# Edge MLP of a four-layer graph network: the stages of TensorE moved two groups apart, with two PSUM banks each, and another release for the gathers on GpSimd

## Chip, cores and metric

One core of one Trainium2 chip runs the whole program. The metric is the device time of one execution in microseconds (us); the figure for a kernel is the median over several executions.

## What is computed

The reference runs four graph layers over 6250 nodes (128 features) and 100000 edges sorted by destination. After each layer comes a residual sum and a layer norm. The change touches the third layer only, the edge MLP:

```
row, col = src, dst
e = silu(concat(h[row], h[col]) @ We1 + be1)     # 256 -> 64
e = silu(e @ We2 + be2)                          # 64 -> 64
agg = segment_sum(e, row)
out = silu(concat(h, agg) @ Wn1 + bn1) @ Wn2 + bn2
```

## The kernel before, in words

`h @ We1` is done per node ahead of this stage, so for an edge only two table rows are added: one half is looked up by a matmul from a table in SBUF (`look2`, three bf16 parts), the other half is fetched by an indirect DMA from the table `t2` in DRAM. The stage works in groups of eight tiles of 128 edges. There are 98 groups of tiles to gather (`CTILE_GROUPS`) and 104 groups of steps to compute (`CSTEP_GROUPS`), because a tile that spans two windows of nodes is used in more than one step. The gathered rows lie in a ring of 12 groups (`CRING`); a row of the ring may be overwritten once the step group five back (`LAG`) has read it. The engines run the same list of groups, each in its own order, and are held together by semaphores alone:

- **GpSimd (POOL)**, L1798 to L1809: for each tile group it waits for a semaphore `l2_placed`, then for the landing of the group two back (`landed`, L1776), and then issues eight indirect DMAs (L1804).
- **VectorE (DVE)**, L1928 to L1974: `hot_look` (L1931, one tensor_scalar in bf16 of 1024 columns) makes the one-hot matrix for the lookup; `before_silu` (L1942, eight additions) waits for the gather of its group and adds it to the looked-up half; `hot_sum` (L1948, one tensor_tensor in f32 of 1024 columns, both inputs in SBUF) makes the one-hot matrix for the sums; `add` (L1958) adds a window of sums to the accumulator.
- **TensorE (PE)**, L1866 to L1921: `own_half` (L1873, 24 matmuls in bf16), `turn` (L1883, four transposes), `second_product` (L1888 for the bias, L1892 for the product), `summed` (L1899 to clear the window, L1904 for the sums, L1906 to close).
- **ScalarE (ACT)**, L1825 to L1860: `silu1` (L1834), `keep_silu1` (L1839), the second silu (L1847), and the copies that place the indices of a later group (L1826, L1829), after which `l2_placed` rises.
- **SyncE (SP)**, L1812 to L1821: loads the rows for `hot_look`, two groups at a time.

`conv_rounds` (L1766) writes the first round of twelve groups out, puts the full rounds in a hardware loop, and writes out what remains. The order within a step is written by hand. Before, in step k:

```
PE:   own_half(k+2), turn(k+1), second_product(k), summed(k-1)
ACT:  silu1(k+1), keep_silu1(k+1), second silu(k), place(k+6)
DVE:  hot_look(k+3), before_silu(k+2), hot_sum(k), add(k-1)
```

`turn` and `second_product` have one PSUM bank each (`ST`, `EB`), `own_half` and `summed` two each. The next stage starts when the last step of all engines is done. The graph convolutions (`convolution`, L2176) use `conv_rounds` and `landed` too.

Of the kernel before, what the change touches and what calls it, by code (L numbers as in the profile page):

```python
# [21 lines left out]
ACT = mybir.ActivationFunctionType  # L22
# [18 lines left out]
CG = 8  # L41
CRING = 12
CSLOTS = CG * CRING
CSTEP_GROUPS = STEPS // CG
CTILE_GROUPS = -(-ET // CG)
CROUNDS = CSTEP_GROUPS // CRING
LAG = -(-(CSLOTS - CG - USED) // CG)
# [45 lines left out]
def build(nc, x, edge_i, edge_f, W_att_w, W_att_b, W1_w, W1_b, W2_w, W2_b, a_vec,  # L93
# [3 lines left out]
    with ctx:  # L97
# [63 lines left out]
        junk = sb("junk", [P, 2, G * D])  # L161
# [5 lines left out]
        ident = sb("ident", [P, P])  # L167
# [27 lines left out]
        we2 = sb("we2", [P, P])  # L195
# [44 lines left out]
        at = [0]  # L240
# [6 lines left out]
        bias2 = tab_rows(CG * EH // 2, 3).bitcast(BF16)  # L247
# [1515 lines left out]

        def conv_rounds(eng, body, groups):  # L1766

            for g in range(CRING):
                body(0, g, g)
            with eng.Fori(1, groups // CRING) as i:  # L1770
                for g in range(CRING):
                    body(i, g, i * CRING + g)
            for k in range(groups // CRING * CRING, groups):
                body(k // CRING, k % CRING, k)

        def landed(pool, i, g, k):  # L1776
# [5 lines left out]
        def at_least(eng, signal, k, more):  # L1782

            if not isinstance(k, int) or k + more > 0:
                eng.wait_ge(signal, k + more)
# [1 line left out]
        (l2_placed, l2_hotT, l2_look, l2_pre, l2_s1, l2_s1T, l2_s1T_kept, l2_e, l2_s2, l2_same, l2_sum, l2_acc) = (  # L1787
            sem(f"l2_{n}") for n in ("placed", "hotT", "look", "pre", "silu1", "silu1T", "silu1T_kept", "e", "silu2", "hot_sum", "sum", "acc"))
        l2_rel_in = [sem(f"l2_rel_in{n}") for n in range(2)]
        LB, ST, EB = bank[0:2], bank[2], bank[4]  # L1790
        with nc.Block() as block:
            def from_group(k, back):

                return 1 + (max(0, k - back) if isinstance(k, int) else k - back)

            @block.gpsimd
            def _(pool):
                def step(i, g, k):  # L1798
                    pool.wait_ge(l2_placed, from_group(k, LAG))
                    landed(pool, i, g, k)  # L1800
                    pool.sem_inc(rounds, 1)
                    for u in range(CG):
                        slot = g * CG + u
                        q_.indirect_dma_start(mlp_ring[:, slot * EH:(slot + 1) * EH], None, t2, bass.IndirectOffsetOnAxis(  # L1804
                            ap=idx_now[:, slot:slot + 1].bitcast(U32), axis=0)).then_inc(conv_gathered[g], 16)

                pool.wait_ge(t2_out[0], 16 * ((NB + 1) // 2))
                pool.wait_ge(t2_out[1], 16 * (NB // 2))
                conv_rounds(pool, step, CTILE_GROUPS)  # L1809
# [13 lines left out]
            @block.scalar  # L1823
            def _(act):
                def place_tiles(k, g):  # L1825
                    return s_.copy(idx_now[:, g * CG:(g + 1) * CG], dst2_t[:, bass.ds(k * CG, CG)])  # L1826

                def place_steps(k, g):
                    return s_.copy(rel_now[:, g * CG:(g + 1) * CG], rel2[:, bass.ds(k * CG, CG)])  # L1829

                def silu1(k, g):
                    act.wait_ge(l2_pre, k + 1)
                    at_least(act, l2_s1T, k, -1)
                    s_.activation(junk[:, g % 2, :], pre_now[:, g % 2, :, :].rearrange("p u f -> p (u f)"), ACT.Silu).then_inc(l2_s1, 1)  # L1834

                def keep_silu1(k, g):
                    act.wait_ge(l2_s1T, k + 1)
                    at_least(act, l2_e, k, -1)
                    s_.copy(s1T[:, g % 2, :], ST).then_inc(l2_s1T_kept, 1)  # L1839

                def step(i, g, k):
                    if not isinstance(k, int) or k + 1 < CSTEP_GROUPS:
                        silu1(k + 1, g + 1)
                        keep_silu1(k + 1, g + 1)
                    act.wait_ge(l2_e, k + 1)
                    at_least(act, l2_sum, k, -1)
                    s_.activation(s2[:, g % 2, :], EB, ACT.Silu).then_inc(l2_s2, 1)  # L1847
                    if not isinstance(k, int) or k + LAG + 1 < CTILE_GROUPS:
                        place_tiles(k + LAG + 1, (g + LAG + 1) % CRING)
                    if not isinstance(k, int) or k + LAG + 1 < CSTEP_GROUPS:  # L1850
                        at_least(act, l2_same, k, LAG + 2 - CRING)
                        place_steps(k + LAG + 1, (g + LAG + 1) % CRING).then_inc(l2_placed, 1)

                for k in range(LAG + 1):
                    place_tiles(k, k)
                    last = place_steps(k, k)
                last.then_inc(l2_placed, 1)
                silu1(0, 0)
                keep_silu1(0, 0)
                conv_rounds(act, step, CSTEP_GROUPS)  # L1860

            @block.tensor
            def _(pe):
                nodes, offsets = ([pe.alloc_register(f"l2_{n}{u}") for u in range(CG)] for n in ("look", "offset"))

                def own_half(k, g):  # L1866
                    pe.reg_load(nodes, step2_node[0:1, bass.ds(k * CG, CG)])
                    pe.wait_ge(l2_hotT, k + 1)
                    at_least(pe, l2_pre, k, -1)
                    for u in range(CG):  # L1870
                        node = pe.snap(nodes[u], min_val=0, max_val=NT - 1)
                        for c in range(3):
                            last = t_.matmul(LB[g % 2][:, u * EH:(u + 1) * EH], hotT8[:, g % 2, u * P:(u + 1) * P],  # L1873
                                             flat(look2[:, bass.ds(node, 1), c * EH:(c + 1) * EH]), start=(c == 0), stop=(c == 2))
                    last.then_inc(l2_look, 1)

                def turn(k, g):
                    pe.wait_ge(l2_s1, k + 1)
                    at_least(pe, l2_s1T_kept, k, 0)
                    pe.sem_inc(rounds, 1)  # L1880
                    for u in range(CG // 2):
                        at = slice(u * P, (u + 1) * P)
                        last = t_.transpose(ST[:, at], junk[:, g % 2, at], ident[:, :])  # L1883
                    last.then_inc(l2_s1T, 1)

                def second_product(k, g):
                    at_least(pe, l2_s2, k, 0)
                    t_.matmul(EB, ones3, bias2, start=True, stop=False)  # L1888
                    pe.wait_ge(l2_s1T_kept, k + 1)
                    for u in range(CG // 2):  # L1890
                        at = slice(u * P, (u + 1) * P)
                        last = t_.matmul(EB[:, at], s1T[:, g % 2, at], we2[:, :], start=False, stop=(u == CG // 2 - 1))  # L1892
                    last.then_inc(l2_e, 1)

                def summed(k, g):
# [10 lines left out]
                    t_.matmul(window[:, 0:2], zeros2[:, 0:P], zeros2[:, 0:2], start=False, stop=True).then_inc(l2_sum, 1)  # L1906

                def step(i, g, k):
                    if not isinstance(k, int) or k + 2 < CSTEP_GROUPS:
                        own_half(k + 2, g + 2)  # L1910
                    if not isinstance(k, int) or k + 1 < CSTEP_GROUPS:
                        turn(k + 1, g + 1)
                    second_product(k, g)
                    if not isinstance(k, int) or k > 0:
                        summed(k - 1, g - 1 + CRING)

                own_half(0, 0)
                own_half(1, 1)
                turn(0, 0)
                conv_rounds(pe, step, CSTEP_GROUPS)  # L1920
                summed(CSTEP_GROUPS - 1, CSTEP_GROUPS - 1)  # L1921

            @block.vector
            def _(dve):
# [18 lines left out]
                    last.then_inc(l2_pre, 1)  # L1943

                def hot_sum(k, g):
                    dve.wait_ge(l2_placed, from_group(k, LAG))
                    at_least(dve, l2_sum, k, -1)
                    v.tensor_tensor(out=hot8[:, g % 2, :, :], in0=iota[:, :].unsqueeze(1).to_broadcast([P, CG, P]),  # L1948
                                    in1=rel_now[:, g * CG:(g + 1) * CG].unsqueeze(2).to_broadcast([P, CG, P]),
                                    op=ALU.is_equal).then_inc(l2_same, 1)  # L1950
# [7 lines left out]
                    v.tensor_add(here, here, bank[6 + g % 2].rearrange("p (t f) -> p t f", t=CG)).then_inc(l2_acc, 1)  # L1958

                def step(i, g, k):  # L1960
                    if not isinstance(k, int) or k + 3 < CSTEP_GROUPS:
                        hot_look(i, g + 3, k + 3)
                    if not isinstance(k, int) or k + 2 < CSTEP_GROUPS:
                        before_silu(i + (g + 2) // CRING, (g + 2) % CRING, k + 2)
                    hot_sum(k, g)
                    if not isinstance(k, int) or k > 0:
                        add(k - 1, g - 1 + CRING)

                for k in range(3):
                    hot_look(0, k, k)  # L1970
                for k in range(2):
                    before_silu(0, k, k)
                conv_rounds(dve, step, CSTEP_GROUPS)
                add(CSTEP_GROUPS - 1, CSTEP_GROUPS - 1)  # L1974
        for k in range(CTILE_GROUPS):
            conv_count[k % CRING] += 16 * CG

# [460 lines left out]
```

## Time and profile before

| | us |
|---|---|
| median of 3 runs | 5702.95 (5699.57 to 5705.49) |
| the profiled execution | 5707.85 |
| its span in the trace | 5706.1 |

| engine | busy us | share of the span |
|---|---|---|
| PE | 3351.8 | 59% |
| PE weight load | 2787.7 | 49% |
| DVE | 2996.6 | 53% |
| ACT | 1491.7 | 26% |
| POOL | 3889.4 | 68% |

The edge MLP's edge stage lies between 2432 and 3507 us of the span. Shares of the whole span say little of it, as the program has many stages with different limits, one after another. The indirect DMAs of a stage count as busy time of POOL for as long as POOL works on issuing them; the transfer itself comes after.

### The profile page before, as it was taken

How to read it: one execution, taken by the hardware profiler on the slowest of the kernel's cores; microseconds unless marked ns; L12 is line 12 of the kernel's file. 1: busy time of each engine (PE TensorE's matmuls, PEld its weight loads, DVE VectorE, ACT ScalarE, POOL GpSimd, SP SyncE). 2: the span in 40 equal slices, each digit the busy share in tenths (PEclk: the TensorE clock that was granted, in tenths of full speed). 3: DMA queues.
4: the chain of work that ended last, by engine and by line, in shares of the span. 5: the costliest groups of instructions: out<-in, count | busy, mean ns of one | idle time of the engine just before them, and what ended most of it. 6: DMA issues, size and time to landing. Idle time of an engine off the chain costs nothing. (4 is left out here: it accounts for less than half of the span.)

```text
span 5706.1 us, 80490 instructions
## 1 busy us (share of the span) xinstructions
PE 3351.8 (59%) x17155; PEld 2787.7 (49%) x17156; DVE 2996.6 (53%) x10412; ACT 1491.7 (26%) x5625; POOL 3889.4 (68%) x4054
## 2 busy tenths in 40 slices
PE   4444444366666666779999999444444454444443
PEld 3333333355655556667777777333333343333333
DVE  6887777577777787733333333333333343333335
ACT  2334333345555555511111113100000000000001
POOL 3777777727777777377777770577777747777773
PEclk7555555577788787855555556655555565655555
DMA  4222112224444444121111110111111121111111
GB/s 123 54 53 53 53 53 56 48 62 132 132 130 131 131 132 130 52 61 53 53 53 53 53 53 11 52 53 52 52 52 52 52 56 53 53 52 52 52 52 52
DMA packets 220198, 386.15 MB, mean 68 GB/s; under 512 B 83394, under 2 KB 119824, under 8 KB 219940
## 3 DMA queue, kind: packets, MB, share of 16 engines
q0 software_dynamic: 142944, 296.35, 19.0%
q1 hardware_dynamic: 76996, 86.71, 4.9%
q8 instruction: 119, 1.95, 0.1%
q14 instruction: 139, 1.14, 0.1%
HBM read 356.23 MB, written 26.56 MB: 67 GB/s over the span
## 5 line engine op out<-in xcount | busy, mean ns | idle before, releaser
L2187 POOL DMA_INDIRECT arena<-table_gcn,idx_now x1568 | 1491.1, 951 | 717.0 <-issue 418.4
L2234 PE MATMUL pair<-arena,hotf 128*128 x3328 | 755.6, 419 | 1095.3 <-DMA arena<-table_gcn,idx_now 1094.0
L2234 PEld LDWEIGHTS pair<-arena,hotf 128*128 128x128 f32 x3328 | 705.6, 322 | 1240.0 <-issue 1239.9
L655 POOL DMA_INDIRECT arena<-table_attention,idx_now x832 | 811.9, 976 | 271.1 <-issue 193.2
L655 POOL DMA_INDIRECT arena<-table_key_value,idx_now x832 | 788.7, 948 | 276.3 <-issue 220.6
L2261 DVE TENSOR_TENSOR acc<-acc,pair 128x1024 f32 x208 | 253.8, 1220 | 1342.5 <-PE pair L2237 1342.4
L1804 POOL DMA_INDIRECT arena<-table_edge_mlp,idx_now x784 | 754.9, 963 | 261.5 <-issue 214.0
L1043 PE MATMUL pair<-wide,hotf 128*128 128x130 f32 x1664 | 430.9, 439 | 630.4 <-ACT wide L1007 620.9
L1043 PEld LDWEIGHTS pair<-wide,hotf 128*128 128x128 f32 x1664 | 369.1, 326 | 695.5 <-ACT wide L1007 685.8
L2196 ACT COPY idx_now<-src_t 128x8 int32 (+1 forms) x204 | 39.3, 197 | 1876.9 <-PE pair L2237 1865.7
L1942 DVE TENSOR_TENSOR hot<-pair,arena 128x64 f32<-128x64 f32 x832 | 134.0, 224 | 640.0 <-DMA arena<-table_edge_mlp,idx_now 619.1
L1376 PE MATMUL pair<-wide,hotf 128*128 128x132 f32 x1664 | 316.3, 349 | 231.6 <-DVE acc L1406 231.6
L2251 DVE TENSOR_SCALAR hotf<-iota,rel_now,ew_now 128x128 f32<-128x128 f32 x1664 | 444.8, 367 | 7.4 <-ACT ew_now L2201 7.4
L1376 PEld LDWEIGHTS pair<-wide,hotf 128*128 128x128 f32 x1664 | 269.5, 243 | 271.9 <-issue 269.8
L1904 PEld LDWEIGHTS pair<-wide,hotf 128*128 128x128 f32 x1664 | 359.4, 328 | 45.0 <-issue 45.0
L1904 PE MATMUL pair<-wide,hotf 128*128 128x64 f32 x1664 | 378.9, 422 | 0.0
L1367 PE MATMUL pair<-arena 128*128 x1664 | 312.1, 351 | 8.7 <-DVE arena L1423 8.5
L1367 PEld LDWEIGHTS pair<-arena 128*128 128x128 f32 x1664 | 297.5, 268 | 9.2 <-issue 9.2
L1319 ACT ACTIVATE junk<-iota,rel_now 128x128 f32<-128x128 f32 x832 | 265.7, 390 | 18.3 <-ACT idx_now L643 12.6
L1007 ACT ACTIVATE wide<-arena,small 128x129 f32<-128x129 f32 x832 | 267.0, 393 | 0.0
L918 DVE SCALAR_TENSOR_TENSOR junk<-iota,rel_now,arena 128x128 f32<-128x128 f32 x832 | 256.9, 344 | 0.0
L1438 DVE TENSOR_TENSOR junk<-pair,arena 128x512 f32<-128x512 f32 x208 | 143.8, 691 | 204.5 <-DMA arena<-table_key_value,idx_now 204.4
(366 smaller groups left out, 5586.6 us busy)
## 6 DMA issues: line engine op xcount, KB each, us to landing
key<-rel_dram SPq DMA_DIRECT2D x104, 256.0 KB, 3.5
arena<-rel_dram SPq DMA_DIRECT2D x52, 512.0 KB, 3.7
arena<-table_gcn,idx_now POOLq DMA_INDIRECT x1568, 2.5
arena<-table_attention,idx_now POOLq DMA_INDIRECT x832
arena<-table_key_value,idx_now POOLq DMA_INDIRECT x832
arena<-table_edge_mlp,idx_now POOLq DMA_INDIRECT x784, 2.4
table_attention<-arena SPq DMA_DIRECT2D x13, 512.0 KB, 2.9
table_gcn<-acc SPq DMA_DIRECT2D x26, 256.0 KB, 2.3
```

Of the source, the lines that this page charges most:

```text
L655: q_.indirect_dma_start(ring[:, slot, 0:width], None, table, bass.IndirectOffsetOnAxis(ap=idx_now[:, slot:slot + 1].bitcast(U32), axis=0)) ...
L918: last = v.scalar_tensor_tensor(out=junk[:, 0, u * P:(u + 1) * P], in0=iota[:, :], scalar=rel_now[:, g * G + u:g * G + u + 1], in1=dst_sco ...
L1007: last = s_.activation(wide[:, g, u, 0:D + 1], ring[:, g * G + u, 0:D + 1], ACT.Identity, scale=small[:, g, u:u + 1])
L1043: last = t_.matmul(bank[2 * (g % 2) + u // 2][:, (u % 2) * AW:(u % 2) * AW + D + 2], hotf[:, g, u, :], wide[:, g, u, 0:D + 2], start=True, ...
L1319: last = s_.activation(away[:, u * P:(u + 1) * P], iota[:, :], ACT.Abs, scale=-1.0, bias=rel_now[:, g * G + u:g * G + u + 1])
L1367: last = t_.matmul(QB[g % 2][:, u * P:(u + 1) * P], hotT_f[:, g, u * P:(u + 1) * P], flat(look[:, bass.ds(nodes[u], 1), :]), start=True, s ...
L1376: last = t_.matmul(bank[SUM + 2 * (g % 2) + u // 2][:, (u % 2) * AW:(u % 2 + 1) * AW], hotf[:, g, u, :], wide[:, g, u, :], start=True, sto ...
L1804: q_.indirect_dma_start(mlp_ring[:, slot * EH:(slot + 1) * EH], None, t2, bass.IndirectOffsetOnAxis(ap=idx_now[:, slot:slot + 1].bitcast(U ...
L1904: t_.matmul(window[:, bass.ds(offset * EH, EH)], hot8[:, g % 2, u, :], s2[:, g % 2, u * EH:(u + 1) * EH], start=False, stop=False)
L2187: q_.indirect_dma_start(conv_ring[:, slot * D:(slot + 1) * D], None, table, bass.IndirectOffsetOnAxis(ap=idx_now[:, slot:slot + 1].bitcast ...
L2234: t_.matmul(window[:, bass.ds(offset * D, D)], hot8[:, g % 2, u, :], conv_ring[:, bass.ds(slot * D, D)], start=False, stop=False)
L2251: last = v.tensor_scalar(out=hot8[:, g % 2, u, :], in0=iota[:, :], scalar1=rel_now[:, at], scalar2=ew_now[:, at], op0=ALU.is_equal, op1=AL ...
```

## The change

PE's four parts stand two groups apart in place of one; `ST` and `EB` become two banks each, taken in turn; ACT and DVE follow with their own order. Indices are placed eight groups ahead (`PLACED`) in place of six, and POOL waits for `l2_pre` (the additions of L1942 of the group five back) in a wait of its own. On DVE `before_silu` now comes first in a step and `hot_look` second, in front of `hot_sum`; its last loop round is written out. In step k after the change:

```
PE:   own_half(k+4), turn(k+2), second_product(k), summed(k-2)
ACT:  keep_silu1(k+2), second silu(k), silu1(k+4), place(k+8)
DVE:  before_silu(k+4), hot_look(k+6), hot_sum(k), add(k-2)
```

```diff
-        def conv_rounds(eng, body, groups):
+        def conv_rounds(eng, body, groups, unrolled_rounds=0):
...
-            with eng.Fori(1, groups // CRING) as i:
+            looped = groups // CRING - unrolled_rounds
+            with eng.Fori(1, looped) as i:
...
-            for k in range(groups // CRING * CRING, groups):
+            for k in range(looped * CRING, groups):
...
-        LB, ST, EB = bank[0:2], bank[2], bank[4]
+        LB, ST, EB = bank[0:2], bank[2:4], bank[4:6]
+        PLACED = 8
...
-                    pool.wait_ge(l2_placed, from_group(k, LAG))
+                    pool.wait_ge(l2_placed, from_group(k, PLACED - 1))
+                    if not isinstance(k, int) or k >= LAG:
+                        pool.wait_ge(l2_pre, k - LAG + 1)
...
+                    if not isinstance(k, int) or k + 2 < CSTEP_GROUPS:
+                        keep_silu1(k + 2, g + 2)
                     act.wait_ge(l2_e, k + 1)
                     at_least(act, l2_sum, k, -1)
-                    s_.activation(s2[:, g % 2, :], EB, ACT.Silu).then_inc(l2_s2, 1)
+                    s_.activation(s2[:, g % 2, :], EB[g % 2], ACT.Silu).then_inc(l2_s2, 1)
+                    if not isinstance(k, int) or k + 4 < CSTEP_GROUPS:
+                        silu1(k + 4, g + 4)
+                    if not isinstance(k, int) or k + PLACED < CTILE_GROUPS:
+                        place_tiles(k + PLACED, (g + PLACED) % CRING)
...
-                for k in range(LAG + 1):
+                for k in range(PLACED):
                     place_tiles(k, k)
                     last = place_steps(k, k)
...
-                    at_least(pe, l2_s1T_kept, k, 0)
+                    at_least(pe, l2_s1T_kept, k, -1)
...
-                    at_least(pe, l2_s2, k, 0)
+                    at_least(pe, l2_s2, k, -1)
...
+                    if not isinstance(k, int) or k + 4 < CSTEP_GROUPS:
+                        own_half(k + 4, g + 4)
                     if not isinstance(k, int) or k + 2 < CSTEP_GROUPS:
-                        own_half(k + 2, g + 2)
-                    if not isinstance(k, int) or k + 1 < CSTEP_GROUPS:
-                        turn(k + 1, g + 1)
+                        turn(k + 2, g + 2)
                     second_product(k, g)
-                    if not isinstance(k, int) or k > 0:
-                        summed(k - 1, g - 1 + CRING)
+                    if not isinstance(k, int) or k >= 2:
+                        summed(k - 2, g - 2 + CRING)
...
-                    if not isinstance(k, int) or k + 3 < CSTEP_GROUPS:
-                        hot_look(i, g + 3, k + 3)
-                    if not isinstance(k, int) or k + 2 < CSTEP_GROUPS:
-                        before_silu(i + (g + 2) // CRING, (g + 2) % CRING, k + 2)
+                    if not isinstance(k, int) or k + 4 < CSTEP_GROUPS:
+                        before_silu(i + (g + 4) // CRING, (g + 4) % CRING, k + 4)
+                    if not isinstance(k, int) or k + 6 < CSTEP_GROUPS:
+                        hot_look(i, g + 6, k + 6)
                     hot_sum(k, g)
-                    if not isinstance(k, int) or k > 0:
-                        add(k - 1, g - 1 + CRING)
+                    if not isinstance(k, int) or k >= 2:
+                        add(k - 2, g - 2 + CRING)
...
-                conv_rounds(dve, step, CSTEP_GROUPS)
-                add(CSTEP_GROUPS - 1, CSTEP_GROUPS - 1)
+                conv_rounds(dve, step, CSTEP_GROUPS, 1)
+                for k in range(CSTEP_GROUPS - 2, CSTEP_GROUPS):
+                    add(k, k)
```

## Rows read from the trace of the kernel before

**Rows 1.** Stretches: length; busy PE, PEld, DVE, ACT, POOL; PEclk, DMA share, GB/s

```profile
2434.00:3430.00 996.00, 905.38 (x5329) 738.22 (x5330) 341.66 (x1064) 193.17 (x483) 754.93 (x784) 0.51 0.20 54
3430.00:3507.00 77.00, 73.45 (x397) 60.48 (x395) 27.66 (x80) 12.80 (x24) 0.00 (x0) 0.50 0.02 8
```

**Rows 2.** The gathers' line L1804: duration min/median/max, then what POOL waited for

```profile
L1804 POOL DMA_INDIRECT arena<-table_edge_mlp,idx_now x784: 940/944/1994, 2434.2 to 3426.8; - x196
...
  issue: 214.0, 702
  DMA arena<-table_edge_mlp,idx_now: 24.7, 81
```

**Rows 3.** Waits of the stage, 2420 to 3470 us: total, times, longest

```profile
DVE hot L1942 <- DMA arena<-table_edge_mlp,idx_now: 619.1, 96, 8.7
...
PE pair L1883 <- ACT junk L1834: 83.1, 82, 5.7
```

**Rows 4.** Timeline of ACT, the first of the copies that place indices: start, duration

```profile
2431.98 0.20 ACT L1826 COPY idx_now<-tab 128x8 int32<-128x8 int32 x1 [1.65 <-PEq L1529]
```

**Rows 5.** Timeline of POOL and DVE, an ordinary group

```profile
3389.30 1.28 DVE L1942 TENSOR_TENSOR hot<-pair,arena 128x64 f32<-128x64 f32 x8 [6.42 <-DMA arena<-table_edge_mlp,idx_now]
3390.43 0.94 POOL L1804 DMA_INDIRECT arena<-table_edge_mlp,idx_now  x1 [0.30 <-issue]
3390.50 1.22 DVE L1948 TENSOR_TENSOR hotf<-iota,rel_now 128x1024 f32<-128x1024 f32 x1
...
3391.68 0.94 POOL L1804 DMA_INDIRECT arena<-table_edge_mlp,idx_now  x1 [0.30 <-issue]
3392.24 0.64 DVE L1931 TENSOR_SCALAR hotT<-arena,part 128x1024 bf16<-128x1024 bf16 x1
```

**Rows 6.** The same timeline where a gather is stretched: two groups

```profile
2557.56 1.22 DVE L1948 TENSOR_TENSOR hotf<-iota,rel_now 128x1024 f32<-128x1024 f32 x1
2558.31 1.29 POOL L1804 DMA_INDIRECT arena<-table_edge_mlp,idx_now  x1 [0.30 <-issue]
...
2617.53 1.22 DVE L1948 TENSOR_TENSOR hotf<-iota,rel_now 128x1024 f32<-128x1024 f32 x1
2617.57 1.99 POOL L1804 DMA_INDIRECT arena<-table_edge_mlp,idx_now  x1 [0.30 <-issue]
```

**Rows 7.** Timeline: hot_look straight behind the additions, in the first groups

```profile
2456.91 0.94 POOL L1804 DMA_INDIRECT arena<-table_edge_mlp,idx_now  x1 [0.30 <-issue]
2456.94 0.48 DVE L1931 TENSOR_SCALAR hotT<-arena,part 128x1024 bf16<-128x1024 bf16 x1
```

**Rows 8.** Timeline behind the last gather: DVE and PE

```profile
3431.01 1.28 DVE L1942 TENSOR_TENSOR hot<-pair,arena 128x64 f32<-128x64 f32 x8 [8.02 <-DMA arena<-table_edge_mlp,idx_now]
...
3433.09 1.09 PE L1883 MATMUL pair<-ident,junk 128*128 128x128 f32 x4 [2.39 <-ACT junk L1834]
...
3433.93 0.48 DVE L1931 TENSOR_SCALAR hotT<-arena,part 128x1024 bf16<-128x1024 bf16 x1
...
3434.33 1.13 DVE L1942 TENSOR_TENSOR hot<-pair,arena 128x64 f32<-128x64 f32 x8
```

**Rows 9.** Timeline of PE, one step of the end

```profile
3461.79 0.60 PE L1888 MATMUL pair<-tab 3*128 3x512 bf16 x1
...
3464.33 0.60 PE L1899 MATMUL pair<-wide 1*128 1x512 bf16 x1
...
3468.59 1.46 PE L1873 MATMUL pair<-arena,hotT 128*128 x24
```

**Rows 10.** PE's groups of instructions from 3431 to 3507 us

```profile
L1904 PE MATMUL pair<-wide,hotf 128*128 128x64 f32 x144 | 33.1, 425 | 0.0
L1892 PE MATMUL pair<-we,tab 128*128 128x128 f32 x64 | 16.6, 441 | 0.0
```

**Rows 11.** Timeline of the transposes of the next stage, at either clock level

```profile
3508.68 1.12 PE L2061 MATMUL pair<-ident,x_nodes 128*128 128x128 f32 x4
...
3520.56 0.60 PE L2061 MATMUL pair<-ident,x_nodes 128*128 128x128 f32 x4
```

More of the change, by code:

```diff
@@ L1838, in keep_silu1 @@
                     at_least(act, l2_e, k, -1)
-                    s_.copy(s1T[:, g % 2, :], ST).then_inc(l2_s1T_kept, 1)
+                    s_.copy(s1T[:, g % 2, :], ST[g % 2]).then_inc(l2_s1T_kept, 1)
                 def step(i, g, k):
-                    if not isinstance(k, int) or k + 1 < CSTEP_GROUPS:
-                        silu1(k + 1, g + 1)
-                        keep_silu1(k + 1, g + 1)
+                    if not isinstance(k, int) or k + 2 < CSTEP_GROUPS:
+                        keep_silu1(k + 2, g + 2)
                     act.wait_ge(l2_e, k + 1)
                     at_least(act, l2_sum, k, -1)
-                    s_.activation(s2[:, g % 2, :], EB, ACT.Silu).then_inc(l2_s2, 1)
[L1848 to L1852, printed above, removed]
-                for k in range(LAG + 1):
+                    s_.activation(s2[:, g % 2, :], EB[g % 2], ACT.Silu).then_inc(l2_s2, 1)
[3 more added lines that the diff above has]
+                        place_tiles(k + PLACED, (g + PLACED) % CRING)
+                    if not isinstance(k, int) or k + PLACED < CSTEP_GROUPS:
+                        at_least(act, l2_same, k, PLACED + 1 - CRING)
+                        place_steps(k + PLACED, (g + PLACED) % CRING).then_inc(l2_placed, 1)
+                for k in range(PLACED):
                     place_tiles(k, k)
@@ L1858, in _ @@
                 silu1(0, 0)
+                silu1(1, 1)
                 keep_silu1(0, 0)
+                silu1(2, 2)
+                keep_silu1(1, 1)
+                silu1(3, 3)
                 conv_rounds(act, step, CSTEP_GROUPS)
@@ L1882, in turn @@
                         at = slice(u * P, (u + 1) * P)
-                        last = t_.transpose(ST[:, at], junk[:, g % 2, at], ident[:, :])
+                        last = t_.transpose(ST[g % 2][:, at], junk[:, g % 2, at], ident[:, :])
                     last.then_inc(l2_s1T, 1)
                 def second_product(k, g):
-                    at_least(pe, l2_s2, k, 0)
-                    t_.matmul(EB, ones3, bias2, start=True, stop=False)
+                    at_least(pe, l2_s2, k, -1)
+                    t_.matmul(EB[g % 2], ones3, bias2, start=True, stop=False)
                     pe.wait_ge(l2_s1T_kept, k + 1)
@@ L1891, in second_product @@
                         at = slice(u * P, (u + 1) * P)
-                        last = t_.matmul(EB[:, at], s1T[:, g % 2, at], we2[:, :], start=False, stop=(u == CG // 2 - 1))
+                        last = t_.matmul(EB[g % 2][:, at], s1T[:, g % 2, at], we2[:, :], start=False, stop=(u == CG // 2 - 1))
                     last.then_inc(l2_e, 1)
@@ L1908, in step @@
                 def step(i, g, k):
+                    if not isinstance(k, int) or k + 4 < CSTEP_GROUPS:
+                        own_half(k + 4, g + 4)
                     if not isinstance(k, int) or k + 2 < CSTEP_GROUPS:
-                        own_half(k + 2, g + 2)
-                    if not isinstance(k, int) or k + 1 < CSTEP_GROUPS:
-                        turn(k + 1, g + 1)
+                        turn(k + 2, g + 2)
                     second_product(k, g)
-                    if not isinstance(k, int) or k > 0:
-                        summed(k - 1, g - 1 + CRING)
+                    if not isinstance(k, int) or k >= 2:
+                        summed(k - 2, g - 2 + CRING)
                 own_half(0, 0)
@@ L1919, in _ @@
                 turn(0, 0)
+                own_half(2, 2)
+                turn(1, 1)
+                own_half(3, 3)
                 conv_rounds(pe, step, CSTEP_GROUPS)
-                summed(CSTEP_GROUPS - 1, CSTEP_GROUPS - 1)
+                for k in range(CSTEP_GROUPS - 2, CSTEP_GROUPS):
+                    summed(k, k)
             @block.vector
@@ L1945, in hot_sum @@
                 def hot_sum(k, g):
-                    dve.wait_ge(l2_placed, from_group(k, LAG))
+                    dve.wait_ge(l2_placed, from_group(k, PLACED - 1))
                     at_least(dve, l2_sum, k, -1)
@@ L1960, in step @@
                 def step(i, g, k):
-                    if not isinstance(k, int) or k + 3 < CSTEP_GROUPS:
-                        hot_look(i, g + 3, k + 3)
-                    if not isinstance(k, int) or k + 2 < CSTEP_GROUPS:
-                        before_silu(i + (g + 2) // CRING, (g + 2) % CRING, k + 2)
+                    if not isinstance(k, int) or k + 4 < CSTEP_GROUPS:
+                        before_silu(i + (g + 4) // CRING, (g + 4) % CRING, k + 4)
+                    if not isinstance(k, int) or k + 6 < CSTEP_GROUPS:
+                        hot_look(i, g + 6, k + 6)
                     hot_sum(k, g)
-                    if not isinstance(k, int) or k > 0:
-                        add(k - 1, g - 1 + CRING)
-                for k in range(3):
+                    if not isinstance(k, int) or k >= 2:
+                        add(k - 2, g - 2 + CRING)
+                for k in range(2):
                     hot_look(0, k, k)
-                for k in range(2):
+                for k in range(4):
                     before_silu(0, k, k)
-                conv_rounds(dve, step, CSTEP_GROUPS)
-                add(CSTEP_GROUPS - 1, CSTEP_GROUPS - 1)
+                    hot_look(0, k + 2, k + 2)
+                conv_rounds(dve, step, CSTEP_GROUPS, 1)
+                for k in range(CSTEP_GROUPS - 2, CSTEP_GROUPS):
+                    add(k, k)
         for k in range(CTILE_GROUPS):
```

## The prediction

> **What bounds the kernel now.** I read the page for the place of the stage, then its busy time by stretch, then the waits, then the timeline of a few groups. In the stretch with the gathers POOL is busy 754.9 of 996 us, and PE 905.4 [rows 1]. That looks like a bound on PE, but the waits say otherwise. Of POOL's 783 gaps between gathers (98 groups of eight) 702 are called issue, 214.0 us, and 81 are put down to a landing, 24.7 us: 0.305 us each in both cases [rows 2]. A real wait would make the second kind longer; it doesn't, so POOL never waits after its first start, and it runs at 0.944 + 0.305 = 1.25 us per gather, about 10.0 us per group. DVE waits 619.1 us for landings, and PE waits 83.1 us for the first silu, which hangs on these landings [rows 3]. So POOL sets the pace up to its last gather, 3426.8 + 0.9 us [rows 2]. Behind that PE works off what is left: 73.5 of 77 us busy [rows 1].
>
> This splits the change into three terms: when POOL starts, how fast it runs, and how much PE has left when the last rows have landed.
>
> **Start.** Eight groups of indices are placed before the first signal in place of six: four more copies, each 0.2 us long [rows 4]. ACT's copies can overlap, so this costs between 0 and 0.8 us; I take +0.4. Nothing hides it, as POOL's first gather waits for the last of them.
>
> **POOL's extra wait.** Its wait for `l2_pre` of the group five back was met long ago: DVE adds a group as soon as it lands, and POOL itself waits for the landing of the group two back. Behind it on POOL are the eight gathers, and behind these DVE. The gap at a group's first gather, which holds two waits and an increment, is 0.305 us like the others [rows 2]. A third wait: 0, at most 0.01 us x 98 = 1 us. The index copies are moved from six to eight groups ahead, but now stand behind silu1(k+4), which ACT can only do when group k+4 has landed; POOL asks for group k+8 then four groups later, so 30 us are left. SP's row loads keep their distance of three groups to `hot_look`: 0. DVE's written-out round adds instructions to an engine that waits 619.1 us for landings [rows 3]: 0.
>
> **DVE's new order and POOL.** This is the term that I find largest. An ordinary gather takes 0.944 us, but 784 of them take 754.9, so 754.9 - 740.1 = 14.8 us are stretch [rows 1, 2]. The timeline shows whose. Where a gather starts while `hot_sum` (L1948) is running, it ends 0.81 us after `hot_sum` does: started 0.04 us into it, it takes 1.99 (2617.57 + 1.99 = 2619.56, against 2618.75); started 0.75 into it, 1.29 [rows 6]. Today the phases mostly just miss: over all 98 groups the timeline has 28 stretched gathers, one in a group at most. The additions start when the group lands, `hot_sum` 1.20 us later, 0.07 behind a gather's start; the next gather starts 1.18 into it, when 0.04 is left, and takes 0.94 [rows 5].
>
> After the change `hot_look` stands between. Straight behind the additions it starts at 1.19 and takes 0.48, with a gather started 0.03 before it that keeps its 0.94 [rows 7]; the next DVE instruction follows 0.40 after it [rows 8]. So `hot_sum` starts 1.60 us after the additions, 0.47 after a gather's start at 1.13 [rows 5], and the next gather falls 0.78 into it with 0.44 left. The nearest row is the one started 0.75 into it: 1.29 us, +0.34 [rows 6]. That is for 97 groups (the last has no gather behind it) 33 us. In seven groups of 98 (the first pair of [rows 6] is of one) the landing comes so late that `hot_look` itself starts about 0.55 behind a gather's start and is held, as in the ordinary group of today (0.64 in place of 0.48 [rows 5]); there about 0.96 is lost in place of 0.34, 4 us more. From the 37 goes today's 14.8: **+22 us**. As the loss is what is left of `hot_sum`, each 0.1 us of phase is worth 0.1 us per group, 10 us in all. I take that for both ends, since it is the distance by which today's groups miss: +12 and +32.
>
> The page "SBUF — State Buffer" of the Trainium skill, section "Who interferes with whom", says that a DVE instruction with two SBUF inputs contends with a GpSimd instruction that reads SBUF, and one in a 2-port mode with any, and that the second to come is blocked for the whole of the first. Its first half agrees with the 1.99 [rows 6]; by the second half a gather could be held through `hot_look` too, which is a rival below.
>
> **What PE has left.** PE gains nothing in the stretch of the gathers: its 83.1 us of waiting [rows 3] move from `turn` to `own_half`, which needs the additions of the group two back for its bank. At the end it costs. When group 97 is added (3431.01), PE today has `second_product` 96 to 103, eight of them, and `summed` 95 to 103, nine, before it: 64 and 144 instructions [rows 10], with seven `turn` and five `own_half`. After the change `own_half(99)` waits for that addition, in step 95. Behind it are the same `turn` and `own_half`, but `second_product` 95 to 103 and `summed` 93 to 103: one and two more. A `second_product` is 3464.33 - 3461.79 = 2.54 us, a `summed` 3468.59 - 3464.33 = 4.26 [rows 9], together 11.1. PE starts 2.08 us after the addition today (3433.09 [rows 8]), then about 1.9, behind `hot_look`. **+10.9 us**. Nothing covers it: PE has no gap in that stretch. Second banks for `ST` and `EB` remove no wait there, since PE runs without one: 0.
>
> **Sum.** 0.4 + 22 + 10.9 = +33 us. The profiled execution took 5707.85 us (span 5706.1), 4.9 above the median of the runs; on the median of 5702.95 the sum gives 5736. Own range of this case: 5722 to 5750.
>
> **Rivals.**
> 1. The gathers are stretched no more than today (a gather slips in between `hot_look` and `hot_sum`, or the landing phase moves). For it: 70 of 98 groups miss, mostly by 0.1 us,, so phases are fine things. Against: the stretch follows the phase in every row. Time: 5703 + 11.3 = 5714. Chance 0.12.
> 2. `hot_look`, near a gather, is itself held, until 1.19 us after the gather's start, as where it starts 0.56 behind (3391.68 to 3392.88 [rows 5]). Then `hot_sum` starts just before the next gather, and that takes 1.9: 97 x 0.95 = 92, less 15, plus 11.3: 5791. Against: 0.48 at 0.03 behind the start [rows 7]. Chance 0.05.
> 3. One hold over both DVE instructions: the gather begun at 1.13 waits from 1.20 to 2.82 and takes 0.81 more, 2.5 us in place of 0.94: 97 x 1.56 = 151, less 15, plus 11.3: 5850. Against: that gather keeps 0.94 beside `hot_look` [rows 7]. Chance 0.02. [...]
> 4. The other side: TensorE's granted clock rises from its lower level (1.2 GHz) to its upper (2.4) in PE's last stretch. Four transposes take 1.12 us at the one and 0.60 at the other [rows 11]. That stretch has 73.5 us of PE's work today [rows 1] and 84 with the 10.9 more; it would take 45: 5736 - 39 = 5697, and 5675 together with rival 1. It decides once some 70 of the 84 us run at the upper level. Against: PE was busy without a gap there today, and the granted clock was 0.50 all through [rows 1]. Chance 0.05. The page "TensorE: Matmul & The Clock Gate" of the Trainium skill, section "What's actually happening", says that activity releases the throttle; by this rule today's stretch should have run at the upper level, and it did not.
> 5. The change does nothing that can be seen, the waits and banks being slack on both sides: 5703. Chance 0.04.
>
> **How the numbers follow.** My case has 0.72. A difference under 0.2% (11.4 us) is about what a measurement of this kernel can't tell from none: 5691.5 to 5714.4. Rival 1 lies on that edge, half on each side; rival 4 goes 0.03 to faster and 0.02 to same; rival 5 is same. Faster 0.03, same 0.12, slower 0.85. The range takes my case and rival 1: 5712 to 5752, and leaves out rivals 2 to 5 and the ends of mine, 0.2.
>
> **What would show it.** Right: POOL's first start within 1 us of today's; 784 gathers with a mean near 990 ns and a median near 944, one in eight about 1.28; issue gaps still 0.3; DVE still waiting for landings; PE's wait now at L1873; from the last additions behind a landing to the stage's end 86 in place of 75 us, with 72 instructions of L1892 and 176 of L1904 in it, at a granted clock of 0.50. Wrong: a mean of the gathers at or under 963 ns, waits of POOL on DVE or ACT, or a last stretch of the old length.

## The result and the profile after

The changed kernel took 5746.18 us (median of 6, 5741.98 to 5753.52) against 5703.94 us for the kernel before: ratio 1.0074, 95% interval 1.0062 to 1.0085. It is 42 us slower; the forecast was 33 us slower (5736, range 5712 to 5752). A second measurement on another chip gave 5754.55 against 5708.23, ratio 1.0082 (1.0068 to 1.0096), and there the kernel before compared with itself gave 1.0000 (0.9991 to 1.0009). The profiled execution has a span of 5745.2 us against 5706.1.

Busy time of the changed kernel by stretch: first the gathers, then what follows them (columns: length; busy PE, PE weight load, DVE, ACT, POOL with their counts; granted clock, DMA share, GB/s).

```profile
2437.00:3461.00 1024.00, 991.42 (x5282) 795.73 (x5283) 332.01 (x1059) 179.37 (x474) 783.36 (x784) 0.50 0.19 52
3461.00:3551.00 90.00, 87.81 (x440) 72.31 (x439) 31.08 (x85) 14.85 (x31) 0.00 (x0) 0.50 0.02 7
```

Against [rows 1] the first stretch is 28 us longer and the second 13. POOL's busy time grew by as much as its stretch did, 754.9 to 783.4. The view of the gathers' line (now L1808) shows that nothing but their duration changed:

```profile
L1808 POOL DMA_INDIRECT arena<-table_edge_mlp,idx_now x784: 940/944/1932, 2437.2 to 3458.2; - x196
...
  issue: 220.0, 722
  ACT rel_now L1833: 23.2, 1
  DMA arena<-table_edge_mlp,idx_now: 18.6, 61
```

The gaps are 0.305 us each as in [rows 2], the median is still 944 ns, and there is one real wait, the first. From the first gather's start to the last one's are 1021.0 us in place of 992.6, which is +28.4, and 28.4 is also what the busy time grew by (783.4 - 754.9). The timeline of an ordinary group in the hardware loop shows the stretch:

```profile
2970.76 1.28 DVE L1955 TENSOR_TENSOR hot<-pair,arena 128x64 f32<-128x64 f32 x8 [6.87 <-DMA arena<-table_edge_mlp,idx_now]
2971.90 0.94 POOL L1808 DMA_INDIRECT arena<-table_edge_mlp,idx_now  x1 [0.30 <-issue]
2972.03 0.49 DVE L1944 TENSOR_SCALAR hotT<-arena,part 128x1024 bf16<-128x1024 bf16 x1
2972.43 1.22 DVE L1961 TENSOR_TENSOR hotf<-iota,rel_now 128x1024 f32<-128x1024 f32 x1
2973.14 1.32 POOL L1808 DMA_INDIRECT arena<-table_edge_mlp,idx_now  x1 [0.30 <-issue]
```

The gather that starts beside `hot_look` (L1944) keeps its 0.94, as [rows 7] had it. The next one starts 0.71 us into `hot_sum` (L1961) and ends 0.81 us after it: 2974.46 against 2973.65. That is the rule of [rows 6]. Over the whole stage 91 gathers, in 97 groups that have a next one, start 0.04 to 1.06 us into `hot_sum`, and each of them ends 0.80 to 0.82 us after it; four more take 1.01 to 1.05 us. Before, 28 gathers started there.

The rest lies behind the last gather. The lines are the additions of the last gathered group and the last `add` of the changed kernel, then the last `add` of the kernel before:

```profile
3462.41 0.23 DVE L1955 TENSOR_TENSOR hot<-pair,arena 128x64 f32<-128x64 f32 x1 [8.48 <-DMA arena<-table_edge_mlp,idx_now]
...
3550.03 0.69 DVE L1971 TENSOR_TENSOR acc<-acc,pair 128x512 f32 x1 [3.48 <-PE pair L1915]
```

```profile
3505.90 0.69 DVE L1958 TENSOR_TENSOR acc<-acc,pair 128x512 f32 x1 [3.48 <-PE pair L1906]
```

DVE adds that group 4.2 us after the gather's start, as in [rows 8]; from there to the end of the last `add` (3550.72) it is 88.3 us, before 3506.59 - 3431.01 = 75.6: +12.7. The spans differ by 39.1 us: 28.4 and 12.7, and 3.0 by which the first gather comes later (the stages ahead and the first copies), less some 5 that the stages behind took less.

### The profile page after: what moved, and what is told of

The parts are those of the page before. It is cut to its first block and busy times, and to the rows that moved or that the text cites. A ratio compares the mean times of both kernels' runs of the same rounds, so it can differ in the third digit from the quotient of the medians.

```text
span 5745.2 us, 80504 instructions
## 1 busy us (share of the span) xinstructions
PE 3442.7 (60%) x17155; PEld 2849.1 (50%) x17156; DVE 2990.5 (52%) x10412; ACT 1480.1 (26%) x5627; POOL 3919.8 (68%) x4054
## 5 line engine op out<-in xcount | busy, mean ns | idle before, releaser
L1808 POOL DMA_INDIRECT arena<-table_edge_mlp,idx_now x784 | 783.4, 999 | 261.8 <-issue 220.0
L1882 PE MATMUL pair<-arena,hotT 128*128 x2496 | 275.6, 236 | 29.7 <-DVE hotT L1944 20.9
L1838 ACT ACTIVATE junk<-hot 128x512 f32<-128x512 f32 x104 | 65.6, 630 | 819.3 <-DVE hot L1955 819.3
L1319 ACT ACTIVATE junk<-iota,rel_now 128x128 f32<-128x128 f32 x832 | 265.7, 390 | 18.3 <-ACT idx_now L643 12.6
```

What stands on the lines that cost most here:

```text
L1319: last = s_.activation(away[:, u * P:(u + 1) * P], iota[:, :], ACT.Abs, scale=-1.0, bias=rel_now[:, g * G + u:g * G + u + 1])
```

## The experiments

Twelve runs follow, on four chips, each beside the kernel before on the same chip. On the first two chips every kernel was slow: the kernel before took 6959 and 6970 us. What was slow there is told with the runs; their times say little of this change, but the durations of single gathers say much. On the last two chips the kernel before took 5708 and 5707 us.

### The order on DVE, alone and undone

`e1_look_last` is the changed kernel with `hot_look` at the end of the step:

```diff
-                    if not isinstance(k, int) or k + 6 < CSTEP_GROUPS:
-                        hot_look(i, g + 6, k + 6)
                     hot_sum(k, g)
                     if not isinstance(k, int) or k >= 2:
                         add(k - 2, g - 2 + CRING)
+                    if not isinstance(k, int) or k + 6 < CSTEP_GROUPS:
+                        hot_look(i, g + 6, k + 6)
```

> The changed kernel with one move on DVE: hot_look(k+6) goes from in front of hot_sum to the end of the step. Port theory (the gathers are stretched where hot_sum runs into a gather's start, and hot_look in front of it shifts it there): the phase of before comes back, the 784 gathers sum to about 755 us in place of 783, and the time falls from 5746 by 28 to 5718 (what is left over before is the longer end, 12 us, and at most 2 us because hot_look now comes later behind the last landing). Rival (the gathers slowed for another reason, such as POOL's extra wait or the indices placed eight ahead): gathers stay at 783 us, time stays at 5746.

`e2_before_look_second` is the kernel before with `before_silu(k + 2)` moved in front of `hot_look(k + 3)`:

```diff
-                    if not isinstance(k, int) or k + 3 < CSTEP_GROUPS:
-                        hot_look(i, g + 3, k + 3)
                     if not isinstance(k, int) or k + 2 < CSTEP_GROUPS:
                         before_silu(i + (g + 2) // CRING, (g + 2) % CRING, k + 2)
+                    if not isinstance(k, int) or k + 3 < CSTEP_GROUPS:
+                        hot_look(i, g + 3, k + 3)
```

> The kernel before with one move on DVE: before_silu(k+2) first, hot_look(k+3) second, in front of hot_sum(k). Port theory: the gathers are stretched as in the changed kernel, 755 to about 783 us, nothing else changes: 5704 + 28 = 5732. Rival (the stretch comes from PE's new distances or POOL's release): gathers stay at 755 us, 5704.

The groups of the gathers, first of e1_look_last, then of e2_before_look_second (busy us, mean ns | idle us, what ended it):

```profile
L1808 POOL DMA_INDIRECT arena<-table_edge_mlp,idx_now x784 | 757.5, 966 | 573.7 <-ACT rel_now L1833 306.7 <-issue 261.2 <-DVE hot L1955 4.6
```

```profile
L1804 POOL DMA_INDIRECT arena<-table_edge_mlp,idx_now x784 | 791.6, 1010 | 505.8 <-ACT rel_now L1829 284.0 <-issue 220.6 <-DMA arena<-table_edge_mlp,idx_now 1.2
```

The sums are near the expected ones: 757.5 with the old order in the new kernel (757 expected), 791.6 with the new order in the old kernel (783 expected). Part of that agreement is luck. POOL waits here for other things, so gathers and `hot_sum` meet in other phases than on the first chip: in e2 68 gathers start inside `hot_sum`, not 91, and f5_one_bank_old_release and f6_sum_one_back below, which have the new order too, sum to only 758.8 and 766.1 us. What these traces show is the rule for the single gather: all those that start 0.04 to 1.06 us into `hot_sum` (27 in e1, 68 in e2) end 0.80 to 0.83 us after it. What DVE's order alone costs where POOL sets the pace was not measured. The times, 7013.78 (ratio 1.0077, 1.0057 to 1.0098) and 6975.30 (1.0027, 1.0015 to 1.0039), don't follow the durations, because here POOL has 284 to 307 us of real waits for the placed indices: it does not set the pace. I put the missed times down to that.

### The second input of hot_sum in PSUM

`e3_before_iota_psum` takes away what makes the gather wait, by the theory: `hot_sum` reads `iota` from an unused bank.

```diff
+        l2_iota, iota_p = sem("l2_iota"), bank[3][:, 0:P]
...
-                    v.tensor_tensor(out=hot8[:, g % 2, :, :], in0=iota[:, :].unsqueeze(1).to_broadcast([P, CG, P]),
+                    v.tensor_tensor(out=hot8[:, g % 2, :, :], in0=iota_p.unsqueeze(1).to_broadcast([P, CG, P]),
...
+                v.tensor_copy(iota_p, iota[:, :]).then_inc(l2_iota, 1)
+                dve.wait_ge(l2_iota, 1)
```

> The kernel before with hot_sum's first input (iota, 128 columns) read from an unused PSUM bank in place of SBUF, so that hot_sum has one SBUF input. Port theory (the stretch needs two SBUF inputs): no gather is stretched by hot_sum, the sum of the gathers falls from 755 to about 740 us, time 5704 - 14 = 5690. Rival (any long DVE instruction on SBUF holds the gather, or hot_sum from PSUM is slower and matters): 755 us or more, 5704 or above.

`e4_after_iota_psum` is the same edit in the changed kernel; it also needs `ST` back in one bank, with `at_least(pe, l2_s1T_kept, k, 0)` again.

> The changed kernel with hot_sum's iota in PSUM; for the room, the transposes of the first silu go back to one bank (keep_silu1 waited for one group earlier). Port theory: gathers 783 to about 742 us, time 5746 - 41 = 5705, and what is left against the kernel before with the same edit (5690) is the longer end alone, 12 to 15 us. Rival (the second bank for the transposes matters, or POOL is slowed by something else): more than 5715.

Gathers of e3:

```profile
L1805 POOL DMA_INDIRECT arena<-table_edge_mlp,idx_now x784 | 740.1, 944 | 569.2 <-ACT rel_now L1830 350.3 <-issue 218.3 <-DMA arena<-table_edge_mlp,idx_now 0.6
```

The mean is the unstretched one in both orders, 944 ns in e3 and 946 ns in e4 (741.4 us in all). So it takes the second SBUF input: the same DVE instruction, as long as before but with one input in PSUM, leaves the gathers alone. Times on this chip: ratios 1.0042 (1.0022 to 1.0061) and 1.0103 (1.0083 to 1.0123), again set by something else.

### Four kernels on a second slow chip, and what was slow there

> The changed kernel with hot_look moved behind add, as in e1_look_last, in a second call: there the gathers landed late and set the pace for every kernel (the kernel before took 6959 us). Where the pace is POOL's again (the kernel before near 5704), port theory: gathers 757 us in place of 783, time 5718. Rival (POOL slowed by its wait or by the placing eight ahead): 783 us, 5746. Where landings set the pace again, both give a time above the kernel before, and only the gathers' durations tell.

> The kernel before with hot_sum's iota in PSUM, in a second call. Port theory, where POOL sets the pace: gathers 740 us in place of 755, time 14 us under the kernel before, about 5690, ratio 0.9975. Rival: the removed stretch is eaten by waiting elsewhere, ratio 1.000.

> The changed kernel with PE's summed one group back in place of two (DVE's add stays two back). Tail theory (the work that PE has left behind the last landing costs one for one): one summed less is left, 5746 - 4.3 = 5742, and the stretch from the last additions behind a landing to the last add falls from 88.3 to 84.0 us; gathers unchanged at 783 us. Rival (the distance between the parts buys PE something in the stretch of the gathers): the same or slower than 5746, with PE or POOL waiting there.

The edit of f6_sum_one_back:

```diff
-                    if not isinstance(k, int) or k >= 2:
-                        summed(k - 2, g - 2 + CRING)
+                    if not isinstance(k, int) or k >= 1:
+                        summed(k - 1, g - 1 + CRING)
...
-                for k in range(CSTEP_GROUPS - 2, CSTEP_GROUPS):
-                    summed(k, k)
+                summed(CSTEP_GROUPS - 1, CSTEP_GROUPS - 1)
```

> The changed kernel with one PSUM bank each for the transposes and for the second product, indices placed six groups ahead, and POOL without its wait on l2_pre, as before. My theory (all three cost and give nothing): 5746, gathers 783 us. Rival (POOL's extra wait or the copies ahead cost, or the second banks save): over 5 us to either side.

The edit of f5_one_bank_old_release:

```diff
-        LB, ST, EB = bank[0:2], bank[2:4], bank[4:6]
-        PLACED = 8
+        LB, ST, EB = bank[0:2], [bank[2], bank[2]], [bank[4], bank[4]]
+        PLACED = LAG + 1
...
-                    if not isinstance(k, int) or k >= LAG:
-                        pool.wait_ge(l2_pre, k - LAG + 1)
...
-                    at_least(pe, l2_s1T_kept, k, -1)
+                    at_least(pe, l2_s1T_kept, k, 0)
...
-                    at_least(pe, l2_s2, k, -1)
+                    at_least(pe, l2_s2, k, 0)
```

Against 6970.38 us for the kernel before, f1 took 7030.20 (1.0095), f3 7000.11 (1.0044), f6 7025.69 (1.0083) and f5 7009.91 (1.0061), each within about 0.002. Again no rank follows the gathers, whose sums are 757.2, 740.1, 766.1 and 758.8 us. For f5 and f6 783 us were expected. Only 32 and 37 of their gathers start 0.04 to 1.06 us into `hot_sum`; each of these ends 0.80 to 0.83 us after it. Their questions (one `summed` less at the end; POOL's extra wait, the placing ahead and the second banks) stay open: they need a chip where POOL sets the pace and PE has no gaps behind the last gather, and neither kernel ran on one.

The first expectation above took late landings for what set the pace. The traces say otherwise: in all eight kernels POOL waits 284 to 362 us in this stage for the copies that place indices, and under 2 us for landings. What is late is seen in PE's groups of f3_before_iota_psum, of which `own_half` is shown:

```profile
L1874 PE MATMUL pair<-arena,hotT 128*128 x2496 | 243.4, 236 | 137.4 <-issue 127.6 <-DVE hotT L1932 8.3
```

One matmul of it lasts as long as on the other chips (236 ns against 240), and the granted clock of the whole program is 0.592 against 0.616. But PE idles 308 us over all its groups in gaps that no semaphore explains ("issue"), where the first trace has 6.9 us of it in front of its L1873. I read the chain so: these gaps make PE the late one, ACT places indices late, and POOL waits for them. No run shows it by taking the gaps away, and why PE's instructions come late there wasn't found.

### Both kernels on one chip

> The changed kernel as it is. In the two calls so far the kernel before took 6959 and 6970 us in place of 5704, and PE had gaps in the middle of its groups of matmuls that no semaphore explains. If the chip is as in the first measurement: 5746, ratio 1.0074. If PE is the one that is late (13 us per group in place of 10): the gathers are still stretched to about 780 us, but POOL has time for it, so only the longer end and the different order on PE count; by the four variants run so far (1.006 to 1.010) I expect a ratio of 1.005 to 1.010. Rival: with PE late the distance of two groups between its parts saves waits, ratio below 1.000.

> The kernel before as it is, for its trace on the same chip and for what a comparison of a kernel with itself gives: ratio 1.000 within 0.002. If PE is late: gathers 755 us or a little less, POOL waiting some 300 us for the placing of indices, PE with over 300 us of gaps called issue in the stage, where the first trace has under 15 in front of L1873. Rival (landings late): POOL's waits are for landings and PE's for DVE.

On this chip the kernel before took the time of the first measurement. g_after: 5754.55, ratio 1.0082; g_before: 5708.94 against 5708.23. The gathers of g_after:

```profile
L1808 POOL DMA_INDIRECT arena<-table_edge_mlp,idx_now x784 | 786.9, 1004 | 261.6 <-issue 219.4 <-ACT rel_now L1833 23.0 <-DMA arena<-table_edge_mlp,idx_now 19.2
```

Those of g_before sum to 754.1 us, 962 ns each on average. From first to last gather 1024.6 and 991.8 us, behind the last landing 88.3 and 75.6: the same two terms as in the first pair, 33 and 12.7.

### The square

The kernels of e3 and e4 once more, on a chip where the kernel before takes 5707 us:

> The kernel before with hot_sum's iota in PSUM, again, in the hope of a chip where POOL sets the pace (the last call had one: kernel before 5708). Port theory: gathers 740 us in place of 755, the stage 14 to 15 us shorter, ratio 0.9975, so this beats both kernels. Rival (the time gained at the gathers is lost behind them or in PE): ratio 1.000. If PE is late again (kernel before near 6960): as in the first two calls, 1.004.

> The changed kernel with hot_sum's iota in PSUM (and one bank for the transposes), again. With the run above this makes a square: order of before or after, iota in SBUF or PSUM. If the stretch and the longer end are all there is, the edit takes 41 us off the changed kernel (5708 + 46 - 41 = 5713, ratio 1.001), and 12 to 15 us, the longer end, are left against the kernel before with the same edit. Rival (a third cost of the change, in PE's distances, POOL's release or the placing ahead): a ratio above 1.004. Rival (the edit takes off no more than from the kernel before): 1.0055.

| | iota in SBUF | iota in PSUM |
|---|---|---|
| order of before | 1 (5707) | 0.9977, 0.9968 to 0.9986 (5694.24) |
| order of after | 1.0074 and 1.0082 (5746 and 5755) | 0.9996, 0.9986 to 1.0007 (5706.81) |

Gathers of h_before_psum and h_after_psum:

```profile
L1805 POOL DMA_INDIRECT arena<-table_edge_mlp,idx_now x784 | 741.3, 946 | 261.5 <-issue 210.9 <-DMA arena<-table_edge_mlp,idx_now 27.7 <-ACT rel_now L1830 22.8
```

```profile
L1809 POOL DMA_INDIRECT arena<-table_edge_mlp,idx_now x784 | 741.0, 945 | 261.8 <-issue 211.2 <-DMA arena<-table_edge_mlp,idx_now 27.4 <-ACT rel_now L1834 23.2
```

From first to last gather 979.0 and 978.7 us: with the stretch gone, the two orders run at the same pace, and POOL waits for nothing in either. A group of h_after_psum in the timeline, with the phases of the changed kernel and no stretch:

```profile
2972.83 1.22 DVE L1962 TENSOR_TENSOR hotf<-pair,rel_now 128x1024 f32<-128x1024 f32 x1
2973.48 0.94 POOL L1809 DMA_INDIRECT arena<-table_edge_mlp,idx_now  x1 [0.30 <-issue]
```

The gather starts 0.65 us into `hot_sum` and takes 0.94. In all, 89 gathers of this trace start 0.04 to 1.06 us into `hot_sum`, nearly as many as the 91 of the changed kernel, and none is stretched by it. Behind the last landing are 75.6 us in the one and 88.0 in the other; that 12.4 is nearly the whole difference of the two, 5706.81 - 5694.24 = 12.6. So the change has two costs, and no third that these runs can tell from none: 28 to 33 us at the gathers, about half a percent of the whole, and 12.6 behind them. On these chips the kernel before with `iota` in PSUM beats both kernels, by 13 us and by 52 to 60.

A few gathers above 1 us are left in these two traces (10 and 8). Twelve in all start 0.13 to 0.33 us into `hot_look` and end 0.81 to 0.83 us after that: started 0.13 into it (3213.16 against 3213.03), one takes 1.17. So `hot_look`, a tensor_scalar on bf16 rows in SBUF, stretches a gather by the same rule as `hot_sum`; as it is short and rarely met, this costs about 1 us in each trace.

## Why the prediction was right, point by point

**POOL sets the pace, and the change doesn't touch its waits.** Right: gaps of 0.305 us and one real wait, before and after. The extra wait on `l2_pre`, the placing eight ahead and the second bank of `ST` cost nothing that can be seen: h_after_psum has the first two, lacks the third, and runs its gathers in the 979 us of h_before_psum. The second bank of `EB` and DVE's written-out round are in it too. For the second bank of `ST` it is only the sum that speaks: 28.4 and 12.7 leave 1 of the 42 us. f5_one_bank_old_release, made to test these parts one way, ran on a slow chip alone.

**Start.** +0.4 us was taken. The sixteen copies start 0.1 us apart as the twelve did. The first gather came 3.0 us later in the one pair of traces and 2.7 us earlier in the other, for what lies ahead of the stage, so the sign "within 1 us of today's" failed twice. Counted from the first copy the term is there: 2.58 us to the first gather in `after`, 2.18 in `before` (2437.19 - 2434.61, 2434.16 - 2431.98), and 2.58 and 2.18 on the second chip.

**DVE's new order.** The mechanism was right. That the stretch comes from `hot_sum` and its second SBUF input is shown by the square and by every gather that meets `hot_sum` in eight traces; that DVE's order sets how they meet is read from the timeline. The size was off, +28 (and +33 on the second chip) in place of +22. Of the 97 groups, seven were taken to lose 0.96 us and 90 to lose 0.34, 37 us together. In the trace 15 lose 0.95 (gathers of 1.88 to 1.93 us), and 76 lose 0.38 on average, 43 us together. So the error is mainly the count of the first kind, eight groups too few at 0.6 us each; on the second chip there are 17 of them. The 0.38 has in it that `hot_look` starts 1.19 us behind the start of the additions, as forecast, only in the groups written out; in the hardware loop it is 1.27 (2972.03 - 2970.76 above). In 10 of the 15 groups the additions pause for 0.3 us, as here:

```profile
2939.21 1.13 DVE L1955 TENSOR_TENSOR hot<-pair,arena 128x64 f32<-128x64 f32 x7 [6.88 <-DMA arena<-table_edge_mlp,idx_now]
...
2940.62 0.22 DVE L1955 TENSOR_TENSOR hot<-pair,arena 128x64 f32<-128x64 f32 x1 [0.28 <-issue]
2940.82 0.71 DVE L1944 TENSOR_SCALAR hotT<-arena,part 128x1024 bf16<-128x1024 bf16 x1
2941.46 1.21 DVE L1961 TENSOR_TENSOR hotf<-iota,rel_now 128x1024 f32<-128x1024 f32 x1
2941.59 1.89 POOL L1808 DMA_INDIRECT arena<-table_edge_mlp,idx_now  x1 [0.31 <-issue]
```

The pause of 0.28 us sits inside the additions, and nothing in the trace explains it. `hot_look` now starts 0.48 us behind the start of a gather (2940.34) and is itself held, 0.71 us in place of 0.48, until 1.19 us after that start; `hot_sum` follows just before the next gather. That is the mechanism of rival 2; it is at work in 13 of these 15 groups. The upper end of the term, +32, was set by 0.1 us of phase; the first pair lies within it, the second just above.

**What PE has left.** +10.9 was forecast, 12.7 measured, and 12.4 with `iota` in PSUM. The count was right: 72 instructions of the second product and 176 of the sums fall in that stretch. PE began 2.16 us after the additions, not 1.9. The term that was missing is the first `own_half` behind the wait:

```profile
3464.57 3.37 PE L1882 MATMUL pair<-arena,hotT 128*128 x24 [1.07 <-DVE hotT L1944]
...
3475.64 1.46 PE L1882 MATMUL pair<-arena,hotT 128*128 x24
```

The same 24 matmuls take 3.4 us when PE has just been released for them and 1.5 when their wait had been met long before, +1.9. The stretch with the gathers shows the same: in 62 of the 70 groups of L1882 that the timeline shows there whole, the last matmul ends 3.8 to 4.3 us after the end of the additions it waits for, whether the first starts 0.6 or 2.6 us after them. So their pace counts from the release and not from the moment PE is free; why wasn't looked into. Before, the last wait stood in front of the four transposes, which take 1.1 us either way.

**The sign of PE's wait.** It was expected to turn up as idle time of L1882. It turned up as busy time: 275.6 us for its 2496 matmuls in place of 172.9, and only 29.7 us idle. The rise of PE's busy time in the first stretch, 905 to 991 us, is this, and no work was added.

**The whole.** Both sizes came out low, the gathers by 6 us and the end by 2, and the time landed inside because the range was wide. The ends of the terms add up to 5726 and 5747; the case's own range, 5722 to 5750, goes some 4 us beyond them without a reason given. The measured 5746 lies at the upper end.

**The rivals.** Rival 1 (no more stretch than today) fails by 28 us of gathers. Rivals 2 and 3 need gathers of 1.9 or 2.5 us in every group; 15 of 97 take 1.9 and none more, and the median stretched one takes 1.3. On rival 3 bears what the page "SBUF — State Buffer" of the Trainium skill says in "Who interferes with whom": a DVE instruction in a 2-port mode and one of GpSimd contend, and the first to issue has the shared ports for the whole of its instruction. Which mode `hot_look` runs in no trace shows. A gather that started inside it was held (1.17 us in h_after_psum), which agrees; but a gather that started up to 0.13 us ahead of it kept its 0.94 and `hot_look` its 0.49, so there neither blocked the other for its whole length. Rival 4 (the upper clock level in PE's last stretch) fails: 0.50 granted, with PE busy for 87.8 of 90 us. Rival 5 fails by the ratio.

## What to carry to other kernels

Where GpSimd's issuing of indirect DMAs sets the pace, a long VectorE instruction with two SBUF inputs is here part of the critical path, through its phase against the gathers, although VectorE has two thirds of its time free. Put one of its inputs in PSUM, or look at the timeline for where it falls, before reordering anything around it, and measure: on the slow chips the same edit cost 0.4% (1.0042 and 1.0044). And here a deeper software pipeline on an engine that doesn't set the pace gained nothing per step and paid its depth once, as work left over when the pace-setter was done.

## What the runs showed of the hardware

An indirect DMA of 128 rows takes POOL 0.944 us plus 0.305 to the next. If it starts more than 0.03 us into a DVE tensor_tensor with both inputs in SBUF (0.03 into it took 0.94, 0.04 took 1.99), it can't end before 0.81 us after that instruction; this holds for every such gather of eight traces, slow chips included. With one input in PSUM it isn't held. Started 0.13 to 0.33 us into `hot_look`, a bf16 tensor_scalar of 0.48 us, it is held by the same 0.81.

The page "SBUF — State Buffer" of the Trainium skill, section "Who interferes with whom", says of a `tensor_tensor` that it takes only the read side of the shared ports, while the making of descriptors needs the write side, and gives this as an inferred reason why such an instruction had not stalled a DMA. For an indirect DMA, whose indices lie in SBUF, these runs show a stall (1.99 us for 0.94). That the read of the indices is what waits is my inference.

On two of the chips the program took 22% longer (6959 against 5704 us), with single matmuls and unheld gathers as long as on the others, and with gaps in PE's stream that no semaphore explains. Whether that lies in the chips or in what else went on there isn't known. A gain of a few per thousand on the one kind, 0.9977, was a loss on the other, 1.0042 and 1.0044.
